# Router, shared expert and expert loop in one stage: plain fp32 weights, a new order on TensorE, block owners from partitions

## The reference

```
xf     = layernorm(x)                                # 512 x 512
scores = sigmoid(xf @ gate_weight.T)                 # 512 x 32
sfc    = scores + bias                               # choose with, weigh without
         keep 4 of 8 groups (by the group's largest sfc), then 6 experts among them
tw     = scores of the 6, divided by their sum, times 2.5
routed = sum over the 6 of tw * (silu(xf @ g.T) * (xf @ u.T)) @ down.T      # I = 256
shared = (silu(xf @ sg.T) * (xf @ su.T)) @ sd.T                             # 512 hidden
x      = x + routed + shared
```

## Time and profile before

| | us |
|---|---|
| median of 3 runs (1642.81 to 1647.3) | 1643.4 |
| the profiled execution | 1644.29 |
| its span, first to last instruction | 1642.4 |
| PE busy | 1475.2 (90%) |
| DVE busy | 872.8 (53%) |
| POOL busy | 606.2 (37%) |
| ACT busy | 562.3 (34%) |
| mean granted TensorE clock | 0.953 of full |

### The profile page before, as it was taken

One profiled execution on the slowest core, in us unless ns is written; L12 is line 12 of the kernel. 1 busy time (PEld: TensorE's weight loads), 2 busy tenths in 40 slices (PEclk: granted clock), 3 DMA queues, 4 the chain that ended last, 5 costly groups with the idle time before them and its releaser, 6 DMA issues. The chain is left out here.

```text
span 1642.4 us, 23883 instructions
## 1 busy us (share of the span) xinstructions
PE 1475.2 (90%) x8888; PEld 1204.5 (73%) x8888; DVE 872.8 (53%) x2181; ACT 562.3 (34%) x1040; POOL 606.2 (37%) x287
## 2 busy tenths in 40 slices
PE   3399999999999999999999999489994749999994
PEld 3389999989898989898989898346663635555552
DVE  6144555455387655478655478548304634444442
ACT  4033443444443443443443443312122002232321
POOL 5501503303464803455803454336202223434442
PEclk9699999999999999999999999799996869999997
DMA  3500102112101112102012100720002079999999
GB/s 113 188 7 26 63 7 62 59 39 89 51 7 61 34 65 93 53 8 61 34 65 93 53 1 1 282 103 1 1 1 110 1 283 333 333 337 341 330 343 293
DMA packets 58064, 181.68 MB, mean 111 GB/s; under 512 B 6130, under 2 KB 23026, under 8 KB 47860
## 3 DMA queue, kind: packets, MB, share of 16 engines
q1 hardware_dynamic: 47796, 156.28, 26.3%
q0 software_dynamic: 10176, 24.12, 5.9%
HBM read 158.36 MB, written 22.02 MB: 110 GB/s over the span
## 5 line engine op out<-in xcount | busy, mean ns | idle before, releaser
L65 PE MATMUL ps_x<-wkv_hi,c_hi 128*128 128x256 f32 (+1 forms) x832 | 241.6, 290 | 0.0
L67 PE MATMUL ps_x<-wkv_hi,c_lo 128*128 128x256 f32 (+1 forms) x832 | 234.8, 282 | 0.0
L66 PE MATMUL ps_x<-wkv_lo,c_hi 128*128 128x256 f32 (+1 forms) x832 | 234.7, 282 | 0.0
L65 PE MATMUL ps_x<-c_hi,wkv_hi 128*128 128x402 f32 x512 | 196.0, 383 | 35.8 <-POOL c_lo L415 35.8
L412 POOL TENSOR_TENSOR c_hi<-c_raw,ones 128x1608 fp32r<-128x1608 f32 x32 | 91.8, 2870 | 346.2 <-DMA c_raw<-ctxT 346.2
L841 DVE TENSOR_TENSOR pT<-ps_x,pT 128x512 fp32r<-128x512 f32 (+1 forms) x224 | 145.1, 648 | 135.3 <-ACT pT L711 132.7
L711 ACT CAST pT<-ps_x 128x512 fp32r<-128x512 f32 (+1 forms) x224 | 124.6, 557 | 180.7 <-PE ps_x L581 177.6
L67 PE MATMUL ps_x<-c_hi,wkv_lo 128*128 128x402 f32 x512 | 178.0, 348 | 0.0
L66 PE MATMUL ps_x<-c_lo,wkv_hi 128*128 128x402 f32 x512 | 177.8, 347 | 0.0
L65 PEld LDWEIGHTS ps_x<-wkv_hi,c_hi 128*128 128x128 f32 (+1 forms) x832 | 154.1, 185 | 17.1 <-issue 17.1
L692 ACT CAST vv<-ps_x 128x512 fp32r<-128x512 f32 (+1 forms) x112 | 62.1, 554 | 281.4 <-PE ps_x L67 281.4
(11 more groups left out here) (328 smaller groups left out, 2776.5 us busy)
## 6 DMA issues: line engine op xcount, KB each, us to landing
e_w_gu<-w_gu SPq DMA_DIRECT2D x49, 1024.0 KB, 8.4
c_raw<-ctxT SPq DMA_DIRECT2D x32, 804.0 KB, 5.0
e_w_dn<-w_dn SPq DMA_DIRECT2D x48, 512.0 KB, 5.9
x_tok<-slabs SPq DMA_DIRECT2D x13, 1024.0 KB, 4.9
spare<-slabs SPq DMA_DIRECT2D x8, 1024.0 KB, 8.1
qbd_dram<-qbd_all SPq DMA_DIRECT2D x2, 2048.0 KB, 6.9
qbd<-qbd_dram SPq DMA_DIRECT2D x16, 256.0 KB, 4.8
h_late<-slabs SPq DMA_DIRECT2D x4, 1024.0 KB, 15.7
```

The source lines that it names most:

```text
L65: nc.tensor.matmul(out, a_hi, b_hi, start=start, stop=False)
L66: nc.tensor.matmul(out, a_hi, b_lo, start=False, stop=False)
L67: return nc.tensor.matmul(out, a_lo, b_hi, start=False, stop=stop)
```

## The change

`route` and `experts` become one stage, `route_and_experts`, with one block and no barrier between.

- **Plain fp32.** The gate weights, the shared expert's weights, the transposed tokens (`mT`) and the shared hidden layer stay fp32. Each product is one plain matmul. The rounding on ScalarE and the subtractions on GpSimd and VectorE are gone, and the transposed tokens are copied out by ScalarE (two) and VectorE (two).
- **The order on TensorE.** Transposes, logits, shared_up(0), the ranks, the first half of shared_up(1), one matmul for the owners, the second half; then look_up(0) to look_up(4) with the halves of shared_up(2) and shared_up(3) between them, shared_down(0), look_up(5), shared_down(1) to shared_down(3), turn(0), turn(1), gate_up(0), and the loop, which is unchanged.
- **The owners.** Partition j holds block j: one comparison of 32 columns, one sum, one instruction that spreads the result on a diagonal, and a matmul by ones brings all to each partition. The mask is one instruction.
- **SP.** The shared weights' first half is loaded second, its second half after the write of `xm_dram`. The experts' weights are loaded as soon as the tables are done. `acc0`'s first 512 rows are written when `x2` is done, behind the six pairs of weights.
- **GpSimd** clears `zero` (2560 columns) in place of VectorE.
- **VectorE** picks the slots of block r+1 before it takes in the rows of block r.
- Several buffers share memory: the shared weights lie where `y`, `sg` and `t1` and at last the final sums lie, and `mT` where `hid` and `hT` lie.

The code below keeps what the text speaks of. What stood in `route` is printed above, and the parts of its router chain that are not shown here are taken over as they were.

```diff
-def route(nc, a, keep):
+def route_and_experts(nc, a, keep):
 
 
     ident, ones, x2 = keep["ident"], keep["ones"], keep["x"]
+    AHEAD = U
     WG, WE = KD * 2 * I, KD * 2 * I + (I // P) * D
...
+        mix, mix2 = sb("e_mix", [P, U * (D + 2 * I)]), sb("e_mix2", [P, 2 * U * I])
+        y = mix[:, 0:U * D].rearrange("p (u d) -> p u d", u=U)
+        sg, t1 = (mix[:, U * D + U * I * n:U * D + U * I * (n + 1)].rearrange("p (u d) -> p u d", u=U) for n in range(2))
+        hid, hT = (mix2[:, U * I * n:U * I * (n + 1)].rearrange("p (u d) -> p u d", u=U) for n in range(2))
+        part = mix[:, 0:2 * TT * D].rearrange("p (i t d) -> p i t d", i=2, t=TT)
+        out = mix[:, 2 * TT * D:].rearrange("p (t d) -> p t d", t=TT)
+        raw = mix[:].rearrange("p (s n) -> p s n", s=2)
+        mT = mix2[:, 0:KD * T].rearrange("p (k n) -> p k n", k=KD)
+        assert 2 * WE == U * (D + 2 * I) == 3 * TT * D and KD * T <= 2 * U * I
...
+        ended, owns, spread = sb("r_ended", [P, E]), sb("r_owns", [P, 1]), sb("r_spread", [P, P])
+        turns_, nturn_f = sb("r_turns", [P, NBLK // U]), sb("r_nturn", [P, 1])
+        s_sg, s_t1, s_hid = sb("r_sg", [P, 2, T]), sb("r_t1", [P, 2, T]), sb("r_hid", [P, 2, 2, T])
...
@@ -1897,15 +1675,24 @@
                     wait_turn(sp, dn_full, nth(i, r, plus=1 - U))
                 sp.dma_start(w_dn[:, r % U], a["w_dn"][e]).then_inc(dn_loaded[r % U], 16)
 
-            gate_up(0, 0, True)
-            down(0, 0, True)
-            sp.dma_start(a["acc0"][0:T].rearrange("(t p) d -> p t d", p=P), x2[:]).then_inc(acc_begun, 16)
+            sp.dma_start(gate[:], a["gateT"]).then_inc(g_loaded, 16)
+            sp.dma_start(raw[:, 0], a["shared"][0]).then_inc(w_loaded[0], 16)
+            sp.dma_start(bias[:], a["e_bias"].partition_broadcast(P)).then_inc(b_loaded, 16)
+            sp.dma_start(before[:], a["before"]).then_inc(b_loaded, 16)
+            sp.dma_start(slot[:], a["slot"].partition_broadcast(P)).then_inc(b_loaded, 16)
+            sp.dma_start(token[:], a["token"]).then_inc(b_loaded, 16)
+            sp.wait_ge(xm_done, TT)
+            sp.dma_start(a["xm_dram"].rearrange("(t p) d -> p t d", p=P), xm[:]).then_inc(xm_stored, 16)
+            sp.dma_start(raw[:, 1], a["shared"][1]).then_inc(w_loaded[1], 16)
             sp.wait_ge(zero_done, 1)
             sp.dma_start(a["acc1"].rearrange("(t p) d -> p t d", p=P), zero[:]).then_inc(acc_begun, 16)
             sp.dma_start(a["acc0"][T:], zero[:, 0]).then_inc(acc_begun, 16)
-            for r in range(1, U):
+            sp.wait_ge(tables_done, 2)
+            for r in range(U):
                 gate_up(0, r, True)
                 down(0, r, True)
+            sp.wait_ge(x2_done, TT)
+            sp.dma_start(a["acc0"][0:T].rearrange("(t p) d -> p t d", p=P), x2[:]).then_inc(acc_begun, 16)
             gate_up(0, U)
             n = turns(sp)
             with sp.Fori(0, n) as i:
@@ -1915,6 +1702,7 @@
 
             for i in range(2):
                 wait_turn(sp, added[i], n * (16 * U // 2) + 16)
...
                                              in_=y[:, r % U], in_offset=None, compute_op=ALU.add).then_inc(added[r % 2], 16)
 
+            nc.gpsimd.memset(zero[:], 0.0).then_inc(zero_done, 1)
+            pool.wait_ge(xm_stored, 16)
...
                 nc.gpsimd.indirect_dma_start(out=a[f"acc{i}"], out_offset=bass.IndirectOffsetOnAxis(ap=dump_row[:], axis=0),
...
@@ -1958,10 +1749,14 @@
         @block.vector
         def _(dve):
             nc.vector.memset(one[:], 1.0).then_inc(started, 1)
-            nc.vector.memset(zero[:], 0.0).then_inc(zero_done, 1)
-
-            nc.vector.tensor_scalar(dump[:], keep["token"][:, 0:1], float(T), None, ALU.add).then_inc(dump_done, 1)
-            nc.vector.tensor_scalar(undump[:], keep["token"][:, 0:1], -1.0, -float(T), ALU.mult, ALU.add).then_inc(dump_done, 1)
+            nc.vector.memset(onesE[:], 1.0)
+            norm(dve, x2, xm, xm_done)
+            for g in (1, 3):
+                dve.wait_ge(tr_full, g + 1)
+                nc.vector.tensor_copy(mT[:, g], ps[:, g]).then_inc(m_done[1], 1)
+            dve.wait_ge(b_loaded, 64)
+            nc.vector.tensor_scalar(dump[:], token[:, 0:1], float(T), None, ALU.add).then_inc(dump_done, 1)
+            nc.vector.tensor_scalar(undump[:], token[:, 0:1], -1.0, -float(T), ALU.mult, ALU.add).then_inc(dump_done, 1)
             dve.wait_ge(dump_done, 2)
             nc.vector.tensor_copy(dump_row[:], dump[:]).then_inc(dump_done, 1)
 
...
+            def shared_hidden(n):
+
+                s, m = n // 2, n % 2
+                dve.wait_ge(s_sg_done, n + 1)
+                nc.vector.tensor_tensor(s_t1[:, m], ps[:, 4 + 2 * m], s_sg[:, m], ALU.mult).then_inc(s_t1_done, 1)
+                dve.wait_ge(s_t1_done, n + 1)
+                nc.vector.tensor_tensor(s_hid[:, s, m], ps[:, 5 + 2 * m], s_t1[:, m], ALU.mult).then_inc(s_hid_done, 1)
...
+            link(nc.vector.tensor_tensor(sfc[:], score[:], bias[:].unsqueeze(1).to_broadcast([P, TT, E]), ALU.add))
+            link(nc.vector.tensor_reduce(gmax[:], sfc[:].rearrange("p t (g s) -> p t g s", g=NG), AX.X, ALU.max))
+            first(TOPKG, gmax, gtop, ggt, geq, gcum, gleft, gsel, NG)
+            link(nc.vector.tensor_tensor(masked[:].rearrange("p t (g s) -> p (t g) s", g=NG), sfc[:].rearrange("p t (g s) -> p (t g) s", g=NG),
+                                         gsel[:].rearrange("p t g -> p (t g)").unsqueeze(2).to_broadcast([P, TT * NG, GS]), ALU.mult))
+            first(TOPK, masked, etop, egt, eeq, ecum, eleft, esel, E)
...
+            link(nc.vector.tensor_tensor_scan(cblk[:], onesE[:], nblk[:], 0.0, ALU.mult, ALU.add))
+            link(nc.vector.tensor_tensor(base[:], cblk[:], nblk[:], ALU.subtract))
+
+            link(nc.vector.scalar_tensor_tensor(pos[:], base[:].unsqueeze(1).to_broadcast([P, TT, E]), float(P),
+                                                ps[:, 1, E:E * (TT + 1)].rearrange("p (t e) -> p t e", t=TT), ALU.mult, ALU.add))
+            link(nc.vector.scalar_tensor_tensor(pos[:], pos[:], 1.0, esel[:], ALU.add, ALU.mult))
+            link(nc.vector.tensor_scalar(place[:].rearrange("p e t -> p t e"), pos[:], -1.0, None, ALU.add))
+
+            link(nc.vector.tensor_scalar(ended[:], cblk[:], token[:, 0:1], None, ALU.is_le))
+            link(nc.vector.tensor_reduce(owns[:], ended[:], AX.X, ALU.add))
+            nc.vector.tensor_scalar(spread[:], ident[:], owns[:], float(E - 1), ALU.mult, ALU.min).then_inc(spread_done, 1)
+
+            link(nc.vector.tensor_scalar(turns_[:], slot[:, P:P + NBLK:U], cblk[:, E - 1:E], None, ALU.is_lt))
+            link(nc.vector.tensor_reduce(nturn_f[:], turns_[:], AX.X, ALU.add))
+            nc.vector.tensor_copy(nturn_[:], nturn_f[:]).then_inc(tables_done, 1)
+            dve.wait_ge(owner_full, 1)
+            nc.vector.tensor_copy(owner_[:], ps[:, 0, 0:NBLK]).then_inc(tables_done, 1)
+            dve.wait_ge(tables_done, 2)
+            pick_slots(0, 0)
+            shared_hidden(0)
+            shared_hidden(1)
             for r in range(AHEAD):
-                pick_slots(0, r)
+                if r + 1 < AHEAD:
+                    pick_slots(0, r + 1)
                 rows_in(0, r)
+                if r in (2, 4):
+                    shared_hidden(1 + r // 2)
+            for t in range(TT):
+                dve.wait_ge(down_full, t + 1)
+                nc.vector.tensor_tensor(x2[:, t], ps[:, 4 + t], x2[:, t], ALU.add).then_inc(x2_done, 1)
             hidden(0, 0)
             pick_slots(0, AHEAD)
             with dve.Fori(0, turns(dve)) as i:
...
@@ -2034,9 +1921,21 @@
                 act.wait_ge(hT_full, nth(i, r, plus=1))
                 nc.scalar.copy(hT[:, r % U], ps[:, HT, 0:I]).then_inc(hT_done, 1)
 
+            norm_act(act)
+            for g in (0, 2):
+                act.wait_ge(tr_full, g + 1)
+                nc.scalar.copy(mT[:, g], ps[:, g]).then_inc(m_done[0], 1)
+            act.wait_ge(logit_full, 1)
+            nc.scalar.activation(score[:].rearrange("p t e -> p (t e)"), ps[:, 0, 0:TT * E], ACT.Sigmoid).then_inc(score_done, 1)
+            for n in range(4):
+                act.wait_ge(up_full, n + 1)
+                if n >= 2:
+                    act.wait_ge(s_t1_done, n - 1)
+                nc.scalar.activation(s_sg[:, n % 2], ps[:, 4 + 2 * (n % 2)], ACT.Sigmoid).then_inc(s_sg_done, 1)
             turned(0, 0)
             turned(0, 1)
             gates(0, 0)
+            act.wait_ge(tables_done, 2)
             with act.Fori(0, turns(act)) as i:
                 for r in range(U):
                     turned(i, r + 2)
...
                     ins = nc.tensor.matmul(ps[:, DN], hT[:, b, P * m:P * m + P], w_dn[:, b, m], start=(m == 0), stop=(m == I // P - 1))
                 ins.then_inc(dn_full, 1)
 
-            for r in range(AHEAD):
+            def shared_up(n, u):
+
+                s, m = n // 2, n % 2
+                if u == 0:
+                    pe.wait_ge(w_loaded[s], 16)
```

(58 more changed lines are left out.)

319 lines of the change are left out of this document (76 added, 243 removed).

## The result

The change takes the kernel from 1644.26 us (four runs, 1642.81 to 1647.3) to 1601.1 us (four runs, 1600.26 to 1602.62): a ratio of 0.9736, 95% interval 0.9719 to 0.9753. That is 43 us less and lies in the range of the prediction, 4 us above its number. The profiled execution took 1600.43 us, with a span of 1598.5.

A forecast was written before the change was run, and what follows sets the result against it. TensorE bounds the loop, but waits leave holes ahead of it. Step by step the loop's first look_up moves from 1356.44 to 1310.3, 46.1 us; 1644.29 - 46.1 = 1598.2, forecast 1597 since that execution lies 0.9 above the median; range 1589 to 1610.

The forecast's parts named there:

- Norm: Stage start on VectorE: root 0.25 us after the statistics, xm 1.9 us in place of 8.03, done at 1240.4, before 1255.36.
- Logits: TensorE behind the transposes: 32 plain matmul instructions take 5.5 us, done at 1249.9; bounds 3.9 to 7.8 us.
- First shared half against the choice: TensorE's shared_up(0), 6.9 us plus 2.2 for half clock, ends 1259.0, later than VectorE's choice at 1256.9; mask 0.3.
- Plain fp32: Shared products on TensorE: two plain instructions, 0.86 us, replace three fp32r, 0.68; 48 products take 8.6 us more.
- Owners: Behind the ranks: three VectorE instructions take 0.75 us, before 2.3 to the comparison; matmul and copy 0.5, tables at 1266.3.
- The last shared half: Ahead of the shared_downs: five look_ups and four halves end at 1285.9, then VectorE's last hidden piece is exposed for 1.9 us.
- Sum: All steps up to the loop's first look_up: it moves from 1356.44 to 1310.3, a shift of 46.1 us.
- the early weights: SP issues experts' weights 57 us earlier, priced at nothing; rival that they bring gain, under 1589 us, chance 0.02.
- the late `acc0`: Write at about 1303, 7 us ahead of the loop, first scatter at 1320; costed at nothing, as VectorE's lead hides it.
- VectorE slow by itself: Norm and choice: GpSimd not the cause, xm 6.1 us later and choice 4.6 us more, 1608 us; chance 0.04.
- Half clock ahead of the loop: TensorE's 1250 to 1307: half clock in a third gives 1614, in all 1646; chance 0.08 of over 1610, 0.01 no gain.
- The adds: Loop: late-started scatter chain paces bodies; above 7.3 us a body the gain is gone, at 8 it takes 1672; chance 0.02.

The follow-up runs named there:

- e1: Changed kernel with two GpSimd subtractions of zeros put back beside VectorE, at xm and at the choice: 1607.9 us, stage time 7.3 us longer than the changed kernel.
- e2: Changed kernel with a ScalarE copy of the shared weights' first half put back ahead of the norm's square root: 1608.41 us, stage time 6.8 us longer.
- e4: Changed kernel with the old owner comparison of 128x2304 and its sum, without the owner matmul: 1607.24 us, stage time 6.4 us longer.
- e6: Changed kernel with SP loading the experts' weights only behind the last shared_down: 1611.61 us, stage time 9.0 us longer.
- e7: Kernel before the change with only the norm's square root moved ahead of the weight rounding on ScalarE: 1637.19 us, stage time 6.9 us shorter than before.
- f1: Changed kernel with the turns, look_up(5) and gate_up(0) ahead of the shared_downs, VectorE reordered to match: 1591.36 us, stage time 9.0 us shorter than the changed kernel.

## Why the prediction held, and where it was off

Its clock, read against the profile of after, us from the stage's start:

| point | forecast | measured |
|---|---|---|
| `xm` done | 5.5 | 5.5 |
| logits start | 9.5 | 9.5 |
| logits end | 15.0 | 16.3 |
| shared_up(0) ends | 24.1 | 25.3 |
| ranks end | 27.5 | 28.3 |
| tables | 31.4 | 32.5 |
| shared_down(0) starts | 52.9 | 53.6 |
| shared_downs end (next turn starts) | 67.1 | 69.6 |
| gate_up ends | 72.4 | 75.0 |
| first look_up of the loop | 75.4 | 78.0 |

- **Norm** (root 0.25, `xm` 1.9): right, and e1 and e2 show that both reasons were the right ones.
- **Logits**: the term was mis-sized. I took 5.5 us by the pace of the logits before, a mixture of two clocks (1.00 from 1260 to 1262, 0.50 from 1264 to 1268). All 32 ran at half clock, 6.8 us to the next matmul or 0.21 each. The wider bound of 7.8 held that.
- **First shared half against the choice**: right. 9.15 us at TensorE against 9.1, with one start at half clock, and VectorE done before. The mask took 0.29 as said.
- **Plain fp32**: right, 3.68 us for eight instructions of 512 columns with the first at its own length, 3.88 from one look_up to the next.
- **Owners**: right, behind a clock that was 1 us late; e4 priced them at 6.4 us. From the ranks' start to look_up(0) it was 9.9 us for my 10.5. Five look_ups and four halves took 16.7 for my 16.4.
- **The last shared half**: the hidden piece was exposed, 1.80 us against 1.9. The step that failed is what follows: "Four shared_downs and look_up(5): 14.2". The first shared_down started at half clock (5.40 against 3.60) and the whole took 16.0, 1.8 more. I had that loss in the bound, at 2.2 us a time, and not in the sum.
- **Sum**: 1.3 for logits and 1.8 for the shared_downs, less 0.6 between them and 0.1 more behind: 2.6 us, so the shift was 43.5 and not 46.1. That the profiled execution still came out only 2.2 us above my 1598.2 is in part luck: 0.9 more in the tail, but 1.3 less ahead of the stage, where nothing was changed. The medians add 1.6, since I took before's execution as 0.9 above its median, and after's lies 0.7 below its own.
- **What I held at nothing**: the early weights are worth nothing by e6, the late `acc0` too: the first scatter went 87.8 us into the stage (1321.49) for the 85.1 that I gave, late by what the stage was late, and TensorE never waited for it. The tail's 0.9 us more lie in the landing times of DMAs, which I had taken as equal and which vary as much between the runs here.
- **Rivals**: VectorE slow by itself falls with e1. Half clock ahead of the loop is there in part: the earlier trace rows had 0.71, the stage now has 0.87, under the 0.9 that I had set as a sign of error, and it costs 3.1 us beyond my sum rather than the 17 of that rival. (Its worst case should read 1648: 1597 and 51 us.) The adds don't pace the loop: bodies stay at 6.23.

My expectations for e4 and e6 missed for one reason, the half clock behind a hole. The one for e7 missed since I followed only the moved instruction and not what then stood behind the weights on ScalarE.

## What to carry to other kernels

In these traces a hole of 1.8 to 4.1 us on TensorE cost 1.5 to 2.1 times its length, since the work behind it started at half clock (1.80 and 1.8 in after, 3.85 and 1.8 in e4, 4.07 and 4.4 in e6, 3.02 and 1.4 before the loop), while holes of 0.8 us cost no more than themselves. Look for other ready work to put into such a hole before shortening anything (f1: 9 us by order alone, 8 of them at the two holes). A step taken out of a queue uncovers what stood behind it, so follow the next consumer in each queue before pricing the move (e7). And when a VectorE instruction takes ten times its siblings' time, look for a GpSimd instruction that ends with it.
